# One staging copy for two slots of a gather pipeline in a graph network kernel

## What is computed

```
h = relu(layernorm(x))                          # 6250 nodes x 128
h = relu(h @ proj_w.T + proj_b)
for l in range(2):
    trans = einsum('nh,tdh->tnd', h, edge_W[l]) # 8 edge types
    agg = segment_sum(trans[edge_type, src], dst)   # 100,000 edges, sorted by dst
    h = relu(gru_cell(agg, h, ...))
return x + h @ out_w.T + out_b
```

## Time and profile before

| | |
|---|---|
| executions timed alone | 2217.71, 2195.36, 2193.30 us; median 2195.36 |
| profiled execution, first to last instruction (span) | 2243.1 us; the page gives no other time for it |
| TensorE / VectorE / ScalarE / GpSimd busy | 72% / 34% / 24% / 54% of the span |
| mean granted clock of TensorE | 0.846 of full speed |
| gathers | 1212, 119.22 MB, 19.3% of the 16 DMA engines' span |
| HBM | 211.87 MB read, 38.12 MB written |

### The profile page before, as it was taken

How to read it: one execution, slowest core, us unless ns; L and a number is a source line. 1 busy time by engine, 2 the same in 40 slices (tenths; PEclk the granted TensorE clock), 3 DMA queues, 4 the chain that set the end, 5 groups by cost and what they waited for, 6 DMA issues and landing times.

```text
span 2243.1 us, 34109 instructions
## 1 busy us (share of the span) xinstructions
PE 1624.5 (72%) x10492; PEld 1125.6 (50%) x10493; DVE 751.5 (34%) x3350; ACT 527.8 (24%) x1268; POOL 1201.0 (54%) x1282
## 2 busy tenths in 40 slices
PE   6468777786867755777775887778787775767776
PEld 4345444444544544556553544545454454555555
DVE  6544332423222243343334122212322223333433
ACT  5132232404233112222211111111413311122221
POOL 6455555555555554544453555555555555555552
PEclk9689898898889877877787899889888987788888
DMA  6324536262543322222222766664243253222221
GB/s 170 102 61 158 155 100 207 71 217 86 179 132 85 99 63 63 67 60 62 60 64 73 234 227 202 204 227 133 67 113 83 71 148 82 63 68 66 64 64 37
DMA packets 183315, 251.55 MB, mean 112 GB/s; under 512 B 24396, under 2 KB 156641, under 8 KB 183201
## 3 DMA queue, kind: packets, MB, share of 16 engines
q0 software_dynamic: 58176, 119.22, 19.3%
q1 hardware_dynamic: 123041, 130.73, 18.5%
q10 hardware_dynamic: 1984, 0.13, 0.1%
HBM read 211.87 MB, written 38.12 MB: 111 GB/s over the span
## 4 chain that ended last, share of the span: by engine, by line
another core or an unknown queue 35%; PE 33%; issue 11%; DVE 10%; ACT 4%; DVEq 3%; DMA 3%; POOL 1%; SPq 0%; ACTq 0%; POOLq 0%
PE ps L1042 9%; PE ps L1113 6%; PE ps L1019 6%; PE ps L1105 4%; PE ps L980 3%; DMA blocks<-node_table 2%; PE ps L1093 2%; DVE acc L1618 2%; DVE onehot L1541 1%; ACT counts L756 1%; DVE acc L1638 1%; ACT sums_sb L822 1%; DVEq L1611 1%; DVE onehot L1576 1%
## 5 line engine op out<-in xcount | busy, mean ns | idle before, releaser
L589 POOL DMA_INDIRECT gath<-node_table,gidx x1212 | 1165.0, 961 | 997.3 <-ACT gidx L627 532.5
L1042 PE MATMUL ps<-counts,blocks 128*128 128x504 f16 (+3 forms) x1764 | 426.1, 388 | 76.1 <-issue 49.6
L1638 DVE TENSOR_TENSOR acc<-ps,acc 128x16 f32 x864 | 151.1, 175 | 901.5 <-remote 364.6
L822 ACT COPY sums_sb<-ps 128x512 f32<-128x512 f32 x216 | 126.5, 586 | 922.9 <-remote 598.4
L1113 PE MATMUL ps<-sums_sb,wT 128*128 128x128 f32 x1728 | 262.1, 315 | 99.9 <-ACT sums_sb L822 81.8
L1019 PE MATMUL ps<-work 128*128 128x392 bf16 x983 | 224.7, 367 | 147.5 <-ACT counts L756 55.4
L1042 PEld LDWEIGHTS ps<-counts,blocks 128*128 128x128 bf16 x1764 | 173.0, 102 | 280.5 <-issue 102.0
L1113 PEld LDWEIGHTS ps<-sums_sb,wT 128*128 128x128 f32 x1728 | 249.7, 227 | 114.3 <-issue 65.5
L1105 PE MATMUL ps<-onehot,gath 128*128 128x128 bf16 x2592 | 204.3, 230 | 62.5 <-issue 37.7
L1093 PE MATMUL ps<-sums_sb,wT 128*128 128x96 f32 (+1 forms) x1408 | 212.9, 310 | 47.4 <-issue 29.7
L1093 PEld LDWEIGHTS ps<-sums_sb,wT 128*128 128x128 f32 x1408 | 202.8, 224 | 71.0 <-issue 57.2
(11 more groups left out here) (198 smaller groups left out, 867.4 us busy)
## 6 DMA issues: line engine op xcount, KB each, us to landing
blocks<-node_table SPq DMA_DIRECT2D x84, 672.0 KB
kept_counts<-counts SPq DMA_DIRECT2D x28, 882.0 KB
counts<-kept_counts SPq DMA_DIRECT2D x28, 882.0 KB
gath<-node_table,gidx POOLq DMA_INDIRECT x1212
node_table<-gath SPq DMA_DIRECT2D x14, 336.0 KB, 3.2
node_table<-work SPq DMA_DIRECT2D x14, 336.0 KB
counts<-in_x_dram SPq DMA_DIRECT2D x1, 3080.0 KB
out_dram<-counts SPq DMA_DIRECT2D x13, 224.0 KB
```

The costliest lines, as they stand in the source:

```text
L589: nc.gpsimd.indirect_dma_start(out=gath[:, b, j, :], out_offset=None, in_=tables[l], in_offset=bass.IndirectOffsetOnAxis(ap=gidx[:, b, j:j ...
L822: act.copy(n_sb[:, b // 2, b % 2 * BG:(b % 2 + 1) * BG, :], narrow_sums[b % 2]) \
L1042: last = nc.tensor.matmul(head_ps[:, 0:COLS[share]], blocks[:, j % 2, at, part * H:(part + 1) * H], counts[:, a, 0:COLS[share]], start=(i ...
L1638: nc.vector.tensor_tensor(win, narrow_ps[q][:, g * NARROW:(g + 1) * NARROW], win, ALU.add) \
```

## The change

ScalarE stages the indices of two neighbouring slots in one copy of 8 words a partition instead of two of 4, behind the second slot's sums, and raises the semaphore by 2. GpSimd no longer waits for `sums_ready` before a slot's gathers, only for `idx_staged`. This holds in every round of both layers, and for the staging ahead of each layer.

```diff
@@ gather_round (GpSimd) @@
                         pool.wait_ge(es[l]["idx_staged"], k + (b + 1))
-                        pool.wait_ge(es[l]["sums_ready"], k + (b + 1))
                         pool.sem_inc(es[l]["gathers_begun"], 1)
@@ stage_idx (ScalarE) @@
             def stage_idx(l, group, b):
-                act.copy(gidx[:, b, :], srcT[:, ds(group, BG)]).then_inc(es[l]["idx_staged"], 1)
+                act.copy(gidx[:, b:b + 2, :], srcT[:, ds(group, 2 * BG)].rearrange("p (b j) -> p b j", b=2)) \
+                   .then_inc(es[l]["idx_staged"], 2)
@@ ahead of layer 0 (and of layer 1 alike) @@
-            for b in range(SLOTS):
+            for b in range(0, SLOTS, 2):
                 stage_idx(0, HEADS[0] + b * BG, b)
@@ last_round @@
-                        stage_idx(l, GROUPS + b * BG, b)
+                        if b % 2:
+                            stage_idx(l, GROUPS + (b - 1) * BG, b - 1)
@@ update (every other round) @@
-                    stage_idx(l, n * ROUND + (b + SLOTS) * BG, b)
+                    if b % 2:
+                        stage_idx(l, n * ROUND + (b - 1 + SLOTS) * BG, b - 1)
```

## The result

The changed kernel takes **2273.5 us** (median of 6 executions, 2264.4 to 2276.7), the kernel before beside it 2202.6 us (6 executions, 2193.0 to 2217.7). The ratio is 1.0295, interval 1.0254 to 1.0335: **slower by 3%**; the medians lie 71 us apart. The forecast was 2204 us in a range of 2178 to 2247, a change too small to tell, so the measured time lies above the range.

The account below looks back on a forecast made before the run. Handovers were taken to bound the kernel, neither TensorE (72% busy) nor GpSimd (54%) filling it. Copies -3.6, moved gathers +2 and gather rhythm +10 gave +8.4 us on 2195.4: 2204 us, range 2178 to 2247.

Parts of the forecast that it names:

- (a) The copies: ScalarE's staging copies halve, 312 to 156, some 31 us less busy; -3.6 us on the path, bounds 0 and -31.
- rival 4: ScalarE was the hidden bound and all removed copies count: -31 us, 2164 us, -1.4%; chance 0.05.
- (b) The wait on the sums: GpSimd's wait on a slot's sums never ends last by itself, so removing it is priced 0.
- The moved gathers: Slots 0's and 2's gathers start later, mostly still in time for TensorE: +2 us, bounds 0 and +91.
- rival 3: Slots come late to TensorE after all, 0.4 us in each of 76 rounds: +30 us, 2222 us; chance 0.08.
- (c) The rhythm of the gathers: GpSimd's longer runs of gathers may add gaps in TensorE's issue: +10 us, bounds 0 and +72.
- Rival 2: Longer runs starve TensorE's issue, in the head's rounds and merged pairs: +53 us, 2247 us, +2.3%; chance 0.14.
- Rival 1: Only ScalarE's copies count, TensorE's issue gaps don't follow the runs: 2194 us; chance 0.28.
- the rule on instruction fetch: Engines stream instructions, mostly hidden, so TensorE's issue gaps would have nothing to do with gathers; the rhythm term would be 0.
- What I said would show it: Among the signs: GpSimd's waits for staging copies fewer, under 90, and longer, their total near 530 us.
- the setting of old staging times: The trace's staging times set into pairs: pairs run together some 20 times, 130 runs left, +72 us of issue gaps.

Follow-up runs that it names:

- Experiment 2: Changed kernel, but each pair's indices staged in two copies of 4 words, both behind the second slot's sums: 2270.6 us, ratio 1.029 to the kernel before.
- experiment 1: Changed kernel with GpSimd's wait on the sums put back, the single staging copy for two slots kept: 2268.7 us, ratio 1.027 to the kernel before.
- experiment 8: Kernel before without GpSimd's wait on the sums, staging copies untouched; gives the second trace of the old staging: 2199.8 us, ratio 0.995.
- experiment 6: Changed kernel, with GpSimd waiting for the landing of slot 0's gathers, one break a round: 2291.6 us, ratio 1.037 to the kernel before.
- experiment 11: Changed kernel with only slots 0 and 1 staged in one copy, slots 2 and 3 each behind their own sums: 2337.3 us, ratio 1.059 to the kernel before.
- experiment 9: Changed kernel with two gathers a slot in place of four, other instructions kept, result wrong: 1609.7 us, ratio 0.729 to the kernel before.
- experiment 10: Kernel before with two gathers a slot in place of four, other instructions kept, result wrong: 1580.1 us, ratio 0.715.

## Why the prediction was wrong

*(a) The copies.* The count and the size are right, 156 of 201 ns. ScalarE's busy time fell by 12 us and not by 31: many of the copies overlapped their neighbour, as the 0.09 us pieces of the earlier trace rows already said. Experiment 2 puts the copies back and the time does not move (2270.6 against 2273.5), so -3.6 us is no more than noise here, and rival 4 is out.

*(b) The wait on the sums, 0.* Right, by experiments 1 and 8, to within 1%.

*The moved gathers, +2 us.* Right. TensorE waits twice, 15.0 us. The landing, for which I had only bounds of 0 and 7.2 us, can be had from the DMA packets: the last of them ends 1.35 us after the gather's end, so the small end was a fair choice. I had looked for room before use (6 us and more), found it, and let it settle too much: rival 3 is out, yet the kernel is slower.

***(c) The rhythm of the gathers, +10 us.*** This is the step that failed. It priced the longer runs by the wrong quantity. I priced gaps in TensorE's issue, 0 to +72 us, and they went *down*, from 217 us to 162. What the longer runs held up was the hand-over from TensorE to ScalarE and VectorE, which is not in those rows. It had a row of its own in the trace of before, which I did not read: ScalarE's copies of narrow sums, idle until a "remote" release, 598.4 us in 85 places; after it is 679.9 us in 86. And the earlier trace rows had it as 35% of the chain; I added it to "issue" and passed on. All else being near 0, the term is worth some +71 us by the medians. That is its upper bound of +72, by coincidence, since the bound was worked out for another mechanism; and the range stopped at 2247, where the sum with that bound gives 2266. I chose near the lower end "as TensorE's sums have 6 us and more of room": that argument covers late gathers and says nothing about late hand-overs.

*How the pairing does it.* Slots 0's and 1's gathers now start together behind slot 1's sums, as one run of eight of 9.7 us, and slots 2's and 3's behind slot 3's (127 such runs in the trace, 62 before; no run of four, 71 before). It is slot 0's sums that suffer: they are the first after slot 3's copy has started a run. In layer 0's rounds with head work they end, in the middle, 4.6 us into it (half of them 3.6 to 9.1 us), as at 716.41, and 19 of 25 are copied over 1 us late, by 105 us; in the trace of before it is 11 of 25, by 23 us. ScalarE takes its work in order, so the counts that TensorE made behind these sums are copied late too, and where the head work runs TensorE has nothing else to do then: waits for counts 52 to 89 us. Slot 2's sums are hardly held any more. In total the held time of the sums' copies hardly rose (538 to 572 us); what rose is how much of it TensorE waits for, by 70 us, and the granted clock fell in that stage. That TensorE waits more because the hold moved to slot 0 is read from the traces; no experiment moved it alone. Against the second trace of the old staging: copies +70, issue -25, VectorE -36 (90 to 54), other waits +22, busy time +46, together the 77 us between the spans.

*Rival 2* had sign and place right (the head's rounds of layer 0, 70.5 us), and a price of 2247 us near the 2273 measured. Its mechanism, issue that starves, is not what happened in the changed kernel, so the nearness is luck; it is real where runs reach twelve, in experiments 6 and 11. I gave it 0.14. *Rival 1* (2194) is out. (Half of rival 4's way, which the range names as its lower end, is 2180 and not 2178; nothing hangs on it.) What I drew from the rule on instruction fetch, that the gaps have nothing to do with gathers, does not hold here: with every other instruction in place they are 282 us with runs of twelve, 186 with eight and 9 with runs of four at most (where TensorE waits for gathers instead). The page of the Trainium skill ("Runtime: NRT & Kernel Launch", Instruction fetch mechanics) says only that an engine streams its instructions by itself, mostly hidden; whether the gaps are fetches at all, no run here shows.

*What I said would show it.* GpSimd's waits for copies were to be under 90 and near 530 us; they are 142 and 635.7. So the pairs did not run together as the setting of old staging times had it (it gave some 20 mergers; there are 7 runs over eight). Why is not shown; the copies behind slots 1's and 3's sums, which free the pairs, are themselves held by 82 and 146 us.

*What stays open.* Why a run of gathers holds TensorE's signals is not shown, nor whether the matmuls themselves end late, only that the signals are late, from some 2 to 4 us after the gathers start, and until when. A break without a landing wait, which would tell the issue from the flight of the gathers, was not tried. Nor is it shown why the 30 us between experiments 9 and 10 remain; TensorE's waits for counts are 25.3 us in the one and under 10 in the other. That halving the gathers won 624 us says how much hangs on them altogether, not how it divides between held signals, issue and the clock.

## What to carry to other kernels

Before moving what releases a run of indirect gathers, look for readers of TensorE's results that start just after a run ends though their data is older: idle time ended by "remote", or a large unexplained share of the chain, is a cost of the gathers even where no gather is ever late. Then look where each hand-over falls. In these traces it passed freely outside a run and in the first 2 us after the gathers had started again, and was held from some 4 us on until the last landing, longest when it came soon after that point; it costs most where the waiting engine has nothing else to do. Breaks that wait for the landing restart that clock, but they have to be tried: two in a round were worth 2.4 to 3.8% with the old staging and 1.6 to 7.5% with the paired one, by their place; one in a round cost 0.8% with the paired staging; three cost 5.3% with the old and four 10% with the paired one, for then the gathers come late. And when a step's price rests on a quantity chosen from the trace, check that it is the only one that the step moves.

## What the runs showed of the hardware

- With GpSimd in a run of gathers (0.95 us each, 0.30 between), TensorE's signals come up to 14 us late. Sums that ended outside a run were copied without delay (132 of 132 in the two traces, with the run counted until 1.65 us after its last gather). Held ones go some 0.3 us after the last gather's last packet, when its own semaphore is raised (724.42 to 724.46 against 724.45 in the rows above).
- The hold sets in 2 to 4 us after the gathers start following at least 1.7 us of standstill: 20 of 816 sums late before 2 us, 1103 of 1289 after 4 us, over 15 traces.
- The longer runs also slow the issue of matmuls. In the trace of before the issue waits within runs (until 1.65 us after them) are 94 us in 25 runs of twelve, 81 us in 62 runs of eight and 17 us in 71 runs of four. In the wide round of the earlier trace rows TensorE's instructions start in steps of 0.7 us: 917.87, 918.58, 919.29, 919.99.
- TensorE's mean granted clock was 0.82 with half of the change, 0.85 in the changed kernel, 0.88 with two breaks, 0.97 with half of the gathers, for the same 10492 matmuls, whose busy time is 1637, 1641, 1570 and 1397 us. With four breaks it was 0.83, and 1651 us busy.
